# The first attention of a four-layer block and its input loads, rewritten as one pipeline over batches

## The chip, the cores and the metric

The kernel runs on one core of a Trainium2 chip. A time is the device time of one execution in microseconds (us), the lower the better. The core's engines are TensorE (PE; PEld is its weight load), VectorE (DVE), ScalarE (ACT), GpSimd (POOL) and SyncE (SP). SP computes nothing here, it issues DMAs in order from one queue.

## The reference, cut to what matters

The block has four layers of cross-attention and feed-forward. Only the first attention and the load of its inputs are touched. `x` and `ctx_4096` are (8, 128, 512): 8 batches of 128 tokens. There are 32 query heads and 8 key heads of 16 columns, and four query heads share a key head.

```
q = layernorm(x) @ Wq;  k = ctx @ Wk;  v = ctx @ Wv      # 32, 8 and 8 heads of 16
scores = einsum('bhqd,bhkd->bhqk', q, k) * 16 ** -0.5
out = einsum('bhqk,bhkd->bhqd', softmax(scores), v)
x = x + out @ Wo
```

The products want nearly float32 accuracy. So each operand is split into two float16 halves (high, and low = value - high), and a product is three matmuls: high x high, high x low, low x high (`pair_matmul`, L64 to L69).

## The kernel before

The program is a row of stages with a barrier of all engines between them. Two of them matter here.

`load_and_split_context` (L107 to L148) loads the context, already turned, in four cuts of 512 KB and then all of `x` (2 MB) in one DMA (L119, L120). ScalarE writes the high halves (L138), VectorE the low ones (L145), and then takes the statistics of all eight batches of `x`. A barrier ends it.

`attention` with the plan `A0` (L232) is the second. It works in four turns `g`, one for each group of 8 query heads and 2 key heads; in a turn it goes through the 8 batches, so there are 32 steps. Turns 1 and 2 are a hardware loop (`all_turns`, L367). Each engine runs its own `step(g, i)`, and lags set the order: scores of batch i, turned probabilities of batch i-1, values mixed for i-2, output projection for i-3, addition to `x` for i-4. In numbers, per step of 8 heads (two units of 4 heads):

- keys are spread (L437): the 128 rows of a key bank are multiplied by `spread`, so that each head sees only its own 16 rows. VectorE makes `kb_hi`, GpSimd `kb_lo`, 128x1024 each;
- the scores are 3 matmuls of 128x512 for each unit; VectorE takes the maxima (L800), ScalarE the exponentials, head by head with a sum each (L704);
- the probabilities are turned by TensorE, in float32, 4 for each unit (L586), and come out of PSUM as two halves: high by ScalarE (L691), low by VectorE (L782);
- the values are mixed (24 matmuls of 16 columns), VectorE divides by the sums (L845), TensorE turns the result (L615), and its halves (L715, L824) are multiplied by that turn's 128 rows of Wo: one product of 512 columns, added to `x` (L808). So `x` is added to 32 times.

Weights are loaded and split turn by turn (SP: L449 to L454, four DMAs for each turn). The first DMA transposes of the program come in a later attention (`wide_attention`), where SP issues them for queries (L1102), keys (L1107) and probabilities (L1113).

Of the kernel before, what the change touches and what calls it, by code (L numbers as in the profile page):

```python
# [106 lines left out]
def load_and_split_context(K, x_in, ctx_t):  # L107

    nc = K.nc
    with ExitStack() as c:  # L110
        cn = c.enter_context(nc.sbuf_tensor("ctx_nat", [P, KT, B * P], F32))
        x_in_done, const_done = K.sem("x_in"), K.sem("const")
        cut_in = [K.sem(f"ctx_in{k}") for k in range(KT)]
        hi_done = Steps(K.sem("ctx_hi_done"), list(range(KT)))
        with nc.Block() as block:
            @block.sync
            def _(sp):
                for k in range(KT):
                    sp.dma_start(cn[:, k, :], ctx_t[k * P:(k + 1) * P, :]).then_inc(cut_in[k], 16)  # L119
                sp.dma_start(K.x[:, :, :], x_in.rearrange("b s d -> s b d")).then_inc(x_in_done, 16)  # L120
                sp.wait_ge(x_in_done, 16)

            @block.gpsimd
            def _(pool):
                pool.memset(K.ident[:, :], 0.0).then_inc(const_done, 1)
                pool.memset(K.ones[:, :], 1.0).then_inc(const_done, 1)
                pool.memset(K.half[:, :], -0.5).then_inc(const_done, 1)
                pool.memset(K.minus_one[:, :], -1.0).then_inc(const_done, 1)
                pool.wait_ge(const_done, 4)
                pool.affine_select(out=K.ident[:, :], in_=K.ident[:, :], compare_op=ALU.not_equal, fill=1.0,  # L130
                                   base=0, pattern=[[-1, P]], channel_multiplier=1).then_inc(const_done, 1)
                pool.wait_ge(const_done, 5)

            @block.scalar
            def _(act):
                for k in range(KT):
                    act.wait_ge(cut_in[k], 16)
                    act.activation(K.ctx_hi[:, k, :], cn[:, k, :], ACT.Copy).then_inc(hi_done.sem, 1)  # L138

            @block.vector  # L140
            def _(dve):
                for k in range(KT):
                    dve.wait_ge(cut_in[k], 16)
                    dve.wait_ge(hi_done.sem, hi_done.count(k))
                    dve.tensor_tensor(K.ctx_lo[:, k, :], cn[:, k, :], K.ctx_hi[:, k, :], ALU.subtract)  # L145
                dve.wait_ge(x_in_done, 16)
                for b in range(B):
                    K.take_stats(dve, b)  # L148


# [66 lines left out]
class Attention:  # L217


    def __init__(self, name, groups, heads, dim, blocks, rows, per_unit, key_tiles, value_dim, units, banks, plan, ahead):  # L220
        self.name, self.groups, self.heads, self.dim = name, groups, heads, dim
        self.blocks, self.rows = blocks, rows
        self.per_unit, self.units = per_unit, units
        self.key_tiles, self.value_dim = key_tiles, value_dim
        self.banks = banks
        self.plan, self.ahead = plan, ahead
        self.packed = name == "a0"
        self.normed = name == "a2"
# [4 lines left out]

A0 = Attention("a0", 4, 8, 16, 1, 128, 4, 1, 32, 2, dict(made=1, s=2, ot=1, pt=2, o=1, y=1), {
    0: [("k", 1)], 1: [("q", 0, 1)], 2: [("v", 1)], 2.5: ["wo"]}, {
    3.5: ["wk"], 4: ["wq"], 5: [("k", 0)], 6: [("q", 0, 0), "wv"], 7: [("v", 0)]})
A1 = Attention("a1", 4, 4, 96, 4, 96, 2, 2, 96, 2, dict(made=3, s=2, pt=1, o=1, y=1), {
# [4 lines left out]
A2 = Attention("a2", 8, 4, 128, 4, 128, 4, 1, 128, 1, dict(made=3, s=2, pt=1, o=1, y=1), {  # L242
    0: [("q", 2), ("qn", 3)], 1: [("v", 0), ("q", 3)], 2: [("qn", 4)], 2.5: [("wo", 0)],
    3: [("q", 4), ("qn", 5), ("wo", 1), ("qn", 6), ("wo", 2), ("v", 1), ("q", 5), ("wo", 3), ("qn", 7), ("k", 1)],
    3.5: [("q", 6), ("q", 7)]}, {
    3.5: ["wk"], 4: [("kn", 0), ("wq", 0)], 4.5: [("wq", 1)], 5: [("kn", 1), ("wq", 2)], 5.5: [("wq", 3)],
    6: [("qn", 0), ("qn", 1)], 6.5: ["wv"], 7: [("q", 0), ("k", 0), ("qn", 2)], 7.5: [("q", 1)]})


def attention(K, A, wq, wk, wv, wo, mask=None, qw=None, kw=None):  # L250

    nc, N, G, R, D = K.nc, A.name, A.groups, A.rows, A.dim
    T = B * P
    scale = float(D) ** -0.5
    nt = A.key_tiles * B
    lag_turn, lag_mix, lag_out, lag_add = 1, 2, 3, 4
    heads_of = lambda j: range(j * A.per_unit, (j + 1) * A.per_unit)  # L260
    is_turn = lambda g, n: isinstance(g, int) and g == n
    with ExitStack() as c:
        sb = lambda n, shape, dt: c.enter_context(nc.sbuf_tensor(f"{N}_{n}", shape, dt))
        pair = lambda n, shape: (sb(n + "_hi", shape, F16), sb(n + "_lo", shape, F16))
        sem = lambda n: K.sem(f"{N}_{n}")

        if A.packed:
            nq, nk, nv = (sb(n, [P, KT, w], F32) for n, w in (("nq", P), ("nk", A.value_dim), ("nv", A.value_dim)))
            no = sb("no", [P, 1, DIM], F32)
            spread = sb("spread", [P, A.heads, P], F16)  # L270
            kb = [pair(f"kb{i}", [P, A.heads, P]) for i in range(2)]
            o_nat = sb("o_nat", [P, P], F32)
        else:
            nq, nk, nv = (sb(n, [P, KT, w], F32) for n, w in (("nq", A.blocks * R), ("nk", R), ("nv", R)))
            no = sb("no", [R, A.blocks, DIM], F32)
        wq_p, wk_p = pair("wq", [P, KT, A.blocks * R]), pair("wk", [P, KT, R])
        wv_p, wo_p = pair("wv", [P, KT, A.value_dim]), pair("wo", [R, A.blocks, DIM])
        q_p, k_p, v_p = pair("q", [R, A.blocks, T]), pair("k", [R, nt * P]), pair("v", [P, nt, A.value_dim])
        probs = [sb(f"probs{i}", [P, A.units, 512], F32) for i in range(2)]

        normal = probs if A.packed else [sb(f"normal{i}", [P, A.units, 512], F32) for i in range(2)]
        negmax = [sb(f"negmax{i}", [P, A.heads], F32) for i in range(2)]
        recip = [sb(f"recip{i}", [P, A.heads], F32) for i in range(4)]
        total = [sb(f"total{i}", [P, A.heads], F32) for i in range(2)]
        pt_p = [pair(f"pt{i}", [P, A.units, 512]) for i in range(2)]
        o_p = pair("o", [R, A.blocks, P])
        if A.normed:
            mk = sb("mask", [P, P], F32)
            masked = [sb(f"masked{i}", [P, A.heads, P], F32) for i in range(2)]

            k_ss, k_r, q_ss, q_r = (sb(n, [P, w], F32) for n, w in
                                    (("k_ss", B), ("k_r", B), ("q_ss", B * A.heads), ("q_r", B * A.heads)))
            kn, qn = sb("kn", [P, B, P], F32), sb("qn", [P, 2, A.heads, P], F32)
            wcol, wqk = sb("wcol", [P, 2], F32), sb("wqk", [P, 1], F32)

        per_v = 4
        before_turn = [use for i in sorted(A.ahead) for use in A.ahead[i]]
        made = before_turn + [use for i in sorted(A.plan) for use in A.plan[i]]
        prep = [use for use in made if use[0] == "w" or use[0] in ("wq", "wo")]
        last_qkv = [use for use in prep if "wo" not in (use, use[0])][-1]  # L300
        last_wo = [use for use in prep if "wo" in (use, use[0])][-1]
        banked = [use for use in made if use not in prep]
        last_of = lambda kinds, half: [use for use in made if use[0] in kinds and (use in before_turn) == (half == 0)][-1]
        free_banks = iter(K.bank)
        take = lambda name, uses: Banks(K, f"{N}_{name}", [next(free_banks) for _ in range(A.banks[name])], uses)
        units = [(b, j) for b in range(B) for j in range(A.units)]
# [6 lines left out]
        if A.packed:  # L313
            ot_bank = take("ot", list(range(B)))
            every_bank.append(ot_bank)
# [47 lines left out]
        def all_turns(engine, step):  # L363

            for i in range(B):
                step(0, i)
# [2203 lines left out]
```

## Time and profile before

| | us |
|---|---|
| median of 3 runs | 1888.47 (1884.77 to 1889.16) |
| profiled execution, its own time | 1886.01 |
| its span, first to last instruction | 1884.3 |
| loads and context split, with barrier | 0 to about 19.2 |
| first attention up to the first maximum of scores | 19.2 to 51.4 |
| its 32 steps up to the last exponentials | 51.4 to about 258 |
| drain and barrier; the next stage's first VectorE work | 258 to 272.4 |
| everything after, not touched | 272.4 to 1884.3 |

The page gives each engine's busy time over the whole span (PE 1605.5 us, DVE 1178.5, ACT 796.8, POOL 608.8). The touched part is its first seventh, so the stretches and single rows are what to read. A row in order of time gives start, length, engine and line, what was written from what, and in brackets how long the engine had been idle and who ended that. "SPq" is a DMA being issued by SP: its length is the time that SP is held, not that of the transfer.

### The profile page before, as it was taken

To read this page: it belongs to the slowest core of one execution; us is meant where nothing else is said; L and a number is where in the kernel's file an instruction comes from. 1 tells how busy PE (TensorE), PEld (TensorE's weight loads), DVE (VectorE), ACT (ScalarE), POOL (GpSimd) and SP (SyncE) were. 2 spreads that over 40 slices of the span, in tenths; PEclk is the share of its full clock that TensorE was granted. 3 is DMA by queue.
4 is the path that set the end of the run, shared out by engine and by line. 5 is a ranking of instruction groups with operands and counts; after the bars stand their busy time and mean duration, and the time that the engine had idled before them with its cause. 6 is when DMAs were issued, how large, how long until landed. Compare 5 with 4: busy or idle time off the path is not lost. (4 is left out here: it accounts for less than half of the span.)

```text
span 1884.3 us, 31640 instructions
## 1 busy us (share of the span) xinstructions
PE 1605.5 (85%) x10796; PEld 897.1 (48%) x10796; DVE 1178.5 (63%) x2287; ACT 796.8 (42%) x2789; POOL 608.8 (32%) x517
## 2 busy tenths in 40 slices
PE   2888955899899999996699999999996769449997
PEld 1455532344366666652365555555552334234443
DVE  5677776434455555564588887888777879771212
ACT  2676755211044334332176666666652312251111
POOL 2333328100014443450066666666653001220000
PEclk9899976799999999998799999999999779869998
DMA  2000012000034442240264546565433000200001
GB/s 103 15 15 15 1 69 92 0 0 0 1 83 93 78 78 62 57 79 26 94 141 104 132 106 129 105 133 107 99 77 91 34 1 1 62 31 0 0 0 45
DMA packets 265956, 111.07 MB, mean 59 GB/s; under 512 B 232305, under 2 KB 248497, under 8 KB 265698
## 3 DMA queue, kind: packets, MB, share of 16 engines
q1 hardware_dynamic: 265826, 109.40, 25.1%
q8 instruction: 74, 1.21, 0.3%
q14 instruction: 56, 0.46, 0.1%
HBM read 52.74 MB, written 2.10 MB: 29 GB/s over the span
## 5 line engine op out<-in xcount | busy, mean ns | idle before, releaser
L67 PE MATMUL bank<-a_wo_hi,a_o_hi 128*128 128x512 f16 (+1 forms) x416 | 159.1, 382 | 19.1 <-DVE a_o_lo L824 10.4
L1443 POOL TENSOR_TENSOR a_recip<-a_total,minus_one 128x4 f32<-128x4 f32 x96 | 97.8, 1019 | 195.9 <-ACT a_probs L1295 195.9
L69 PE MATMUL bank<-a_wo_hi,a_o_lo 128*128 128x512 f16 (+1 forms) x416 | 159.1, 383 | 0.0
L68 PE MATMUL bank<-a_wo_lo,a_o_hi 128*128 128x512 f16 (+1 forms) x416 | 159.1, 382 | 0.0
L1450 POOL TENSOR_TENSOR a_normal<-a_probs,a_recip 128x512 f32<-128x512 f32 x128 | 155.4, 1224 | 7.5
L1435 POOL TENSOR_TENSOR a_q_ss<-a_q_ss,half 128x4 f32<-128x4 f32 x64 | 89.2, 1393 | 189.3 <-DVE a_q_ss L1365 95.5
L1295 ACT ACTIVATE a_probs<-a_masked,a_negmax 128x128 f32<-128x128 f32 x256 | 99.6, 390 | 94.8 <-DVE a_negmax L1340 94.8
L1306 ACT ACTIVATE a_o_hi<-bank 128x512 f16<-128x512 f32 (+1 forms) x96 | 57.1, 595 | 180.6 <-PE bank L69 180.4
L1558 ACT ACTIVATE f_h_hi<-f_h 128x512 f16<-128x512 f32 (+1 forms) x50 | 31.5, 630 | 205.8 <-DVE f_h L1579 144.1
L67 PE MATMUL bank<-xn_hi,f_w_hi 128*128 (+1 forms) x288 | 110.9, 385 | 8.2 <-PEq L1511 8.2
L437 POOL TENSOR_TENSOR a_kb_lo<-a_k_lo,a_spread 128x1024 f16<-128x1024 f16 x32 | 69.4, 2169 | 150.1 <-PE bank L69 139.5
L68 PE MATMUL bank<-xn_lo,f_w_hi 128*128 (+1 forms) x288 | 110.7, 384 | 0.0
L69 PE MATMUL bank<-xn_hi,f_w_lo 128*128 (+1 forms) x288 | 110.5, 384 | 0.0
L1350 DVE TENSOR_TENSOR a_o_lo<-bank,a_o_hi 128x512 f16<-128x512 f32 (+1 forms) x96 | 65.6, 683 | 67.3 <-ACT a_o_hi L1306 67.3
L67 PE MATMUL bank<-a_wq_hi,xn_hi 128*128 128x512 f16 x256 | 97.3, 380 | 0.4 <-DVE a_qn L1370 0.4
L68 PE MATMUL bank<-a_wq_lo,xn_hi 128*128 128x512 f16 x256 | 97.3, 380 | 0.0
L69 PE MATMUL bank<-a_wq_hi,xn_lo 128*128 128x512 f16 x256 | 97.3, 380 | 0.0
L1570 DVE SCALAR_TENSOR_TENSOR f_h<-bank,f_act 128x512 f32<-128x512 f32 (+1 forms) x22 | 15.2, 691 | 127.8 <-PE bank L69 127.8
L1295 ACT ACTIVATE a_probs<-bank,a_negmax 128x256 f32<-128x256 f32 x128 | 59.0, 473 | 79.3 <-DVE a_negmax L1342 79.3
L704 ACT ACTIVATE a_probs<-bank,a_negmax 128x128 f32<-128x128 f32 x256 | 90.1, 393 | 4.6 <-DVE a_negmax L800 4.5
L1337 DVE TENSOR_TENSOR a_masked<-bank,a_mask 128x512 f32<-128x512 f32 x64 | 44.2, 690 | 73.0 <-PE bank L69 73.0
L67 PE MATMUL bank<-f_w_hi,f_h_hi 128*128 (+2 forms) x200 | 77.0, 385 | 10.2 <-DVE f_h_lo L1583 9.7
(338 smaller groups left out, 4894.4 us busy)
## 6 DMA issues: line engine op xcount, KB each, us to landing
a_nq<-in_L_xattn_Wq SPq DMA_DIRECT2D x8, 1024.0 KB, 5.7
a_no<-in_L_xattn_Wo SPq DMA_DIRECT2D x8, 1024.0 KB, 6.0
f_n<-in_L_ffn_w SPq DMA_DIRECT2D x1, 3584.0 KB, 11.6
f_n<-in_L_ffn_w2t SPq DMA_DIRECT2D x1, 3584.0 KB, 20.2
a_nq<-in_L_xattn_Wq SPq DMA_DIRECT2D x4, 768.0 KB, 4.8
a_no<-in_L_xattn_Wo SPq DMA_DIRECT2D x4, 768.0 KB, 5.7
f_words<-in_L_ffn_w SPq DMA_DIRECT2D x2, 1280.0 KB, 6.0
ctx_nat<-in_ctx_t SPq DMA_DIRECT2D x4, 512.0 KB, 4.9
```

Of the source, the lines that this page charges most:

```text
L67: pe.matmul(out, lh, rh, start=start, stop=False)
L68: pe.matmul(out, lh, rl, start=False, stop=False)
L69: return pe.matmul(out, ll, rh, start=False, stop=stop)
L437: engine.tensor_tensor(kb[b % 2][half][:, :, :], k_p[half][:, b * P:(b + 1) * P].unsqueeze(1).to_broadcast([P, A.heads, P]), spread[:, :, ...
L704: m = act.activation(probs[i % 2][:, j, n * w:(n + 1) * w], src, ACT.Exp, bias=negmax[i % 2][:, h:h + 1], accum_out=total[i % 2][:, h:h + 1])
L1295: m = act.activation(probs[s % 2][:, h, :], src, ACT.Exp, bias=negmax[s % 2][:, h:h + 1], accum_out=total[s % 2][:, h:h + 1])
L1306: act.activation(o_p[s % 2][0][:, :, :], o_bank[s][0:R, :].rearrange("p (h q) -> p h q", h=H), ACT.Copy).then_inc(ohi_done.sem, 1)
L1337: dve.tensor_tensor(masked[s % 2][:, :, :], s_bank[(s, 0)][:, :].rearrange("p (h n) -> p h n", h=H), mk[:, :].unsqueeze(1).to_broadcast([P ...
L1350: dve.tensor_tensor(o_p[s % 2][1][:, :, :], o_bank[s][0:R, :].rearrange("p (h q) -> p h q", h=H), o_p[s % 2][0][:, :, :], ALU.subtract).th ...
L1435: pool.tensor_tensor(r[:, :], r[:, :], K.half[:, 0:n], ALU.pow).then_inc(root_done.sem, 1)
L1443: pool.tensor_tensor(recip[s % 2][:, :], total[s % 2][:, :], K.minus_one[:, :], ALU.pow).then_inc(recip_done.sem, 1)
L1450: m = pool.tensor_tensor(normal[s % 2][:, t, :, :], probs[s % 2][:, :, t * P:(t + 1) * P], by, ALU.mult)
```

## The change

The two stages become one function, `first_attention`. It has no turns: all weights are loaded once, and a flat list of steps `t` from -15 to 89 goes over 64 units (8 batches of 8 units, a unit is 4 heads). Each engine walks the same steps and does at step t what the offsets say (`at(t, offset)` is the batch for which the offset falls on t, `live(t - lag)` the unit).

- Load: `x` and context come batch by batch (256 KB each); GpSimd, which has the constants and the square roots as before, now also takes the low halves of rows, context, keys, probabilities and heads.
- q and k: the host permutes Wq. A batch's queries come out of one bank of 128x512, its keys out of 128x128, which VectorE masks into two copies with alternate 16 rows (`keep`). SP then stacks the halves: 12 DMAs of 32 partitions put (high, low, high) of q below one another in 96 rows of `q3`, 12 more put (high, high, low) of k in `k3`. One matmul over 96 rows then is the whole three-part product of a score.
- Softmax: the values get a 17th column of ones, so that mixing also gives the sums; the exponentials keep none. Probabilities are split before they are turned: high by VectorE (five of eight units) or GpSimd (three of eight), low by GpSimd. SP turns both halves in one DMA transpose (128 x 1024 of float16), as it does for the normalised rows and for the heads.
- Output: all 32 heads of a batch are gathered, divided, split and turned by DMA, and the projection of 4 products goes into one bank. `x` is added to 8 times.

The diff, cut to its core:

```diff
-def load_and_split_context(K, x_in, ctx_t):
...
-def attention(K, A, wq, wk, wv, wo, mask=None, qw=None, kw=None):
...
+def first_attention(K, x_in, ctx_t, keep_in, wq, wk, wv, wo):
...
+    NORM, XHI, XLO, CTX = -15, -15, -13, -12
+    QPROJ, QSPLIT, KPROJ, KMASK, KSPLIT, VPROJ, VSPLIT = -9, -5, -10, -8, -8, -4, -3
+    PHI, PLO, MIX = 2, 2, 7
+    DIVIDE, OSPLIT, OUT, ADD = 11, 17, 22, 26
+    FIRST, END = -15, TOTAL + ADD
...
+    PS, PB = 6, 10
...
+        by_vector = lambda t: t % UNITS not in (2, 5, 7)
...
+                def stack_queries(b):
+                    sp.wait_ge(q_bank.freed(b), q_bank.n_drained(b))
+                    scored(b)
+                    for m in range(4):
+                        for third, half in enumerate((0, 1, 0)):
+                            sp.dma_start(q3[b % 2][32 * third:32 * third + 32, m, :, :].rearrange("p g n -> p (g n)"),
+                                         q_hl[b % 2][32 * m:32 * m + 32, half, :]).then_inc(q3_in[b % 2], 16)
...
+                def turn_probs(t):
+                    sp.wait_ge(plo_done.sem, plo_done.count(t))
+                    if t >= PB:
+                        sp.wait_ge(mixed.sem, mixed.count(t - PB))
+                    sp.dma_start_transpose(p_t[t % PB][:, :, :, :].rearrange("p a h n -> p (a h) n"),
+                                           p_hl[t % PS][:, :, :].rearrange("p a n -> p (a n)")).then_inc(p_in[t % PB], 16)
...
+                for t in range(FIRST, END):
+                    for b in at(t, XLO):
+                        turn_queries_in(b)
+                    for b in at(t, KSPLIT):
+                        stack_keys(b)
...
+                    for u in live(t - PLO):
+                        turn_probs(u)
+                    for b in at(t, OSPLIT):
+                        turn_heads(b)
+                    for b in at(t, QSPLIT):
+                        stack_queries(b)
...
+                def scores(t):
+                    b, i = t // UNITS, t % 4
+                    if t % UNITS == 0:
+                        landed(pe, q3_in, b, 12)
+                        landed(pe, k3_in, b, 12)
+                    pe.wait_ge(s_bank.freed(t), s_bank.n_free(t))
+                    for mm in range(2):
+                        m = 2 * (t % UNITS // 4) + mm
+                        r = pe.matmul(s_bank[t][:, 256 * mm:256 * mm + 256], q3[b % 2][:, m, i, :], k3[b % 2][:, m, :, :],
+                                      start=True, stop=True)
...
+                def high_of_probs(t):
+                    dve.wait_ge(s_bank.freed(t), s_bank.n_drained(t))
+                    if t >= PS:
+                        dve.wait_ge(p_in[(t - PS) % PB], 16 * ((t - PS) // PB + 1))
+                    dve.tensor_copy(p_hl[t % PS][:, 0, :], probs[t % PS][:, :]).then_inc(phi_done[0].sem, 1)
...
+                def low_of_probs(t):
+                    high_ready(pool, t)
+                    pool.tensor_tensor(p_hl[t % PS][:, 1, :], probs[t % PS][:, :], p_hl[t % PS][:, 0, :],
+                                       ALU.subtract).then_inc(plo_done.sem, 1)
...
-        load_and_split_context(K, a["x"], a["ctx_t"])
...
-    attention(K, A0, *(a[f"L0_xattn_{w}"] for w in ("Wq", "Wk", "Wv", "Wo")))
+    first_attention(K, a["x"], a["ctx_t"], a["keep"], *(a[f"L0_xattn_{w}"] for w in ("Wq", "Wk", "Wv", "Wo")))
```

SP before, from the start of the program (L119: context, L449 to L454: the first turn's weights):

```order
L119 DMA ctx_nat<-in_ctx_t 128x1024 x4
L120 DMA x_state<-in_x 128x8x512
L115 UNCONDITIONAL_BRANCH
L442 UNCONDITIONAL_BRANCH
L449 DMA a_nk<-in_L_xattn_Wk 128x4x32
L450 DMA a_nv<-in_L_xattn_Wv 128x4x32
L451 DMA a_nq<-in_L_xattn_Wq 128x4x128
L454 DMA a_no<-in_L_xattn_Wo 128x512
```

SP now, one batch's worth in the middle (`a_p_hl`: halves of the probabilities, `a_o_hl`: of the heads, `a_xn_hl`: of the normalised rows, `a_q_hl` and `a_k_hl`: of q and k):

```order
L300 DMA_TRANSPOSE a_p_t<-a_p_hl 128x8x128 x2
L307 DMA_TRANSPOSE a_o_t<-a_o_hl 128x8x128
L300 DMA_TRANSPOSE a_p_t<-a_p_hl 128x8x128
L272 DMA_TRANSPOSE a_xn_t<-a_xn_hl 128x8x128
L300 DMA_TRANSPOSE a_p_t<-a_p_hl 128x8x128
L285 DMA a_q<-a_q_hl 32x512 x12
L300 DMA_TRANSPOSE a_p_t<-a_p_hl 128x8x128
L314 DMA a_ctx<-in_ctx_t 128x4x128
L300 DMA_TRANSPOSE a_p_t<-a_p_hl 128x8x128 x3
L293 DMA a_k<-a_k_hl 32x256 x12
```

Behind four loads for each turn there now stand, for each batch, 10 transposes, 24 short copies and a load.

VectorE before, one step of 8 heads (L437 spreads keys, L845 divides, L824 and L782 are low halves):

```order
L800 TENSOR_REDUCE a0_negmax0<-bank1 128x4
L800 TENSOR_REDUCE a0_negmax0<-bank2 128x4
L808 SCALAR_TENSOR_TENSOR x_state<-bank6,x_state 128x512
L824 TENSOR_TENSOR a0_o_lo<-bank7,a0_o_hi 128x128
L782 TENSOR_TENSOR a0_pt1_lo<-bank3,a0_pt1_hi 128x512
L782 TENSOR_TENSOR a0_pt1_lo<-bank4,a0_pt1_hi 128x512
L437 TENSOR_TENSOR a0_kb1_hi<-a0_k_hi,a0_spread 128x1024
```

VectorE now, three steps of a middle batch (L558: high half of the probabilities, L564 and L568: divide, L576: high half of the heads, L529: low half of q):

```order
L551 TENSOR_REDUCE a0_negmax1<-bank1 128x4
L576 CAST a0_o_hl0<-a0_o_nat0 128x512
L558 CAST a0_p_hl0<-a0_probs0 128x512
L551 TENSOR_REDUCE a0_negmax2<-bank2 128x4
L580 SCALAR_TENSOR_TENSOR x_state<-bank6,x_state 128x512
L98 BN_STATS stats<-x_state 128x6
L558 CAST a0_p_hl1<-a0_probs1 128x512
L551 TENSOR_REDUCE a0_negmax3<-bank0 128x4
L564 RECIPROCAL a0_recip0<-bank3 128x16
L568 TENSOR_TENSOR a0_o_nat1<-bank3,a0_recip0 128x256
L529 SCALAR_TENSOR_TENSOR a0_q_hl1<-bank5,a0_q_hl1 128x512
```

For each unit the maxima stay; the low halves out of PSUM and the spreading are gone, and copies from SBUF to SBUF have come.

## Rows read from the trace of the kernel before

**Rows 1.** Table of stretches: length, busy us (count) by engine, clock, DMA share.

```profile
0.00:19.20 19.20, 0.00 (x0) 0.00 (x0) 9.74 (x12) 5.51 (x5) 0.93 (x9) 1.00 0.60 218
19.20:51.40 32.20, 16.28 (x108) 8.95 (x109) 15.56 (x38) 7.49 (x21) 9.36 (x7) 0.90 0.12 29
51.40:258.00 206.60, 174.64 (x1777) 102.69 (x1775) 155.84 (x333) 147.14 (x657) 65.15 (x30) 0.93 0.04 10
258.00:272.40 14.40, 7.79 (x68) 3.95 (x68) 8.05 (x17) 2.22 (x7) 0.04 (x1) 0.57 0.00 0
```

**Rows 2.** Order of time, VectorE: start, us, work, idle before it.

```profile
14.15 4.84 DVE L98 BATCH_NORM_STATS2 stats<-x_state 128x6 f32<-128x512 f32 x8 [3.33 <-DMA x_state<-in_x]
...
22.09 5.89 DVE L179 TENSOR_SCALAR a_n_xn<-x_state,a_n_mv,a_n_rstd 128x512 f32<-128x512 f32 x8 [2.14 <-POOL a_n_rstd L186]
```

**Rows 3.** Order of time at the stage's end, VectorE.

```profile
270.63 0.69 DVE L98 BATCH_NORM_STATS2 stats<-x_state 128x6 f32<-128x512 f32 x1
272.40 0.64 DVE L176 BATCH_NORM_AGGREGATE f_n_mv<-stats 128x2 f32<-128x6 f32 x8 [1.08 <-PEq L103]
```

**Rows 4.** Order of time at the stage's end, TensorE.

```profile
264.34 0.61 PE L67 MATMUL bank<-a_wo_hi,a_o_hi 128*128 128x512 f16 x1 [1.04 <-DVE a_o_lo L824]
264.74 0.63 PE L68 MATMUL bank<-a_wo_lo,a_o_hi 128*128 128x512 f16 x1
...
265.67 0.17 PE L68 MATMUL bank<-a_v_lo,a_pt_hi 128*128 128x16 f16 x1
265.69 0.17 PE L69 MATMUL bank<-a_v_hi,a_pt_lo 128*128 128x16 f16 x1
```

**Rows 5.** Order of time, SP queue: three DMA transposes in a row.

```profile
1353.84 1.23 SPq L1102 DMA_TRANSPOSE a_q_t<-a_q_nat  x1
1355.16 1.23 SPq L1107 DMA_TRANSPOSE a_k_t<-a_k_nat  x1
1356.48 1.26 SPq L1113 DMA_TRANSPOSE a_p_t<-a_p_nat  x1
```

**Rows 6.** Order of time, SP queue: short transfers behind one another.

```profile
859.70 0.32 SPq L1848 DMA_DIRECT2D f_nbias<-in_L_ffn_b  x1
860.08 0.36 SPq L1849 DMA_DIRECT2D f_had<-in_hadamard  x1
860.48 0.42 SPq L1850 DMA_DIRECT2D f_na<-in_L_ffn_lora_A  x1
```

**Rows 7.** Order of time, SP queue: a transfer behind four large loads.

```profile
921.52 0.51 SPq L1087 DMA_DIRECT2D a_no<-in_L_xattn_Wo  x1
922.07 1.08 SPq L1092 DMA_DIRECT2D a_mask<-in_mask_1x1xSxS_ff  x1
```

**Rows 8.** Groups by shape, VectorE, 51.4 to 258 us: total, mean ns.

```profile
L800 DVE TENSOR_REDUCE a_negmax<-bank 128x4 f32<-128x512 f32 x64 | 41.1, 680 | 4.0 <-PE bank L69 3.6 <-issue 0.3
```

**Rows 9.** Groups by shape, VectorE, from 300 us on.

```profile
L1370 DVE TENSOR_TENSOR a_kn<-bank,a_k_ss 128x256 f32<-128x256 f32 x32 | 13.6, 425 | 4.7
...
L1985 DVE TENSOR_SCALAR f_te<-f_tw 128x512 int32<-128x512 int32 x12 | 5.1, 427 | 0.4
```

**Rows 10.** Groups by shape, GpSimd, from 300 us on.

```profile
L1453 POOL CAST a_p_nat<-a_normal 128x512 f16<-128x512 f32 x64 | 43.1, 673 | 4.1
...
L2283 POOL TENSOR_TENSOR x_weight<-x_picked,x_recip 128x512 f32<-128x512 f32 x8 | 8.3, 1039 | 74.9 <-DVE x_recip L2257 74.9
```

**Rows 11.** One line's instructions, VectorE: ns min/median/max; a kb_hi product.

```profile
L437 DVE TENSOR_TENSOR a_kb_hi<-a_k_hi,a_spread x32: 676/682/2108, 49.1 to 251.6; 128x1024 f16<-128x1024 f16 x32
```

**Rows 12.** The same for a weight's low half in the later attention.

```profile
L1400 DVE SCALAR_TENSOR_TENSOR a_wk_lo<-a_nk,a_wk_hi x12: 545/1110/1529, 523.2 to 1308.5; 128x512 f16<-128x512 f32 x8, 128x384 f16<-128x384 f32 x4
```

**Rows 13.** DMA issues: KB, median us from issue to landing.

```profile
a_p_t<-a_p_nat SPq DMA_TRANSPOSE x96, 3.2
...
a_nq<-in_L_xattn_Wq SPq DMA_DIRECT2D x4, 256.0 KB, 3.5
```

More of the change, by code:

```diff
@@ L264, in attention @@
         pair = lambda n, shape: (sb(n + "_hi", shape, F16), sb(n + "_lo", shape, F16))
+        ring_of = lambda n, k, shape, dt: [sb(f"{n}{i}", shape, dt) for i in range(k)]
         sem = lambda n: K.sem(f"{N}_{n}")
[L267 to L303, printed above, removed]
@@ L304, in attention @@
-        free_banks = iter(K.bank)
-        take = lambda name, uses: Banks(K, f"{N}_{name}", [next(free_banks) for _ in range(A.banks[name])], uses)
-        units = [(b, j) for b in range(B) for j in range(A.units)]
-        ring, s_bank, pt_bank = take("made", banked), take("s", units), take("pt", units)
-        o_bank, y_bank = take("o", list(range(B))), take("y", list(range(B)))
-        early_units = range(min(A.units, A.banks["pt"]))
-        late_units = range(len(early_units), A.units)
@@ new lines, in first_attention @@
+        units, batches, halves = list(range(TOTAL)), list(range(B)), [(b, hf) for b in range(B) for hf in range(2)]
+        take = lambda name, banks, uses: Banks(K, f"{N}_{name}", banks, uses)
+        s_bank, o_bank = take("s", K.bank[0:3], units), take("o", K.bank[3:5], halves)
+        q_bank, y_bank = take("q", K.bank[5:6], batches), take("y", K.bank[6:7], batches)
+        kv_bank = take("kv", K.bank[7:8], [(kind, b) for b in batches for kind in "kv"])
+        x_here, ctx_here = [sem(f"x_in{b}") for b in batches], [sem(f"ctx_in{b}") for b in batches]
@@ new lines, in first_attention @@
+        w_here = {k: [sem(f"{k}_in{i}") for i in range(4 if k == "wq" else 1)] for k in nat}
+        pieces = [("wk", 0)] + [("wq", i) for i in range(4)] + [("wv", 0)] + [("wo", i) for i in range(4)]
+        whi_done, wlo_done = Steps(sem("whi"), pieces), Steps(sem("wlo"), pieces)
+        per_batch = lambda n: Steps(sem(n), batches)
+        per_unit = lambda n: Steps(sem(n), units)
+        stats_done, mean_done, root_done = sem("stats"), sem("mean"), sem("root")
+        xn_done, xhi_done, xlo_done, chi_done, clo_done = (per_batch(n) for n in ("xn", "xhi", "xlo", "chi", "clo"))
@@ new lines, in first_attention, with landed @@
+        phi_done = [Steps(sem(f"phi{n}"), [u for u in units if by_vector(u) == (n == 0)]) for n in range(2)]
+        high_ready = lambda engine, t: engine.wait_ge(phi_done[not by_vector(t)].sem, phi_done[not by_vector(t)].count(t))
+        weights_at = lambda t: [use for use, when in zip(pieces, WEIGHTS) if when == t]
+        def landed(engine, sems, b, n=1):
+            engine.wait_ge(sems[b % 2], 16 * n * (b // 2 + 1))
+        def weight(use):
+            kind, i = use
+            if kind == "wo":
+                piece = lambda t: t[:, i, :]
+            elif kind == "wq":
+                piece = lambda t: t[:, :, i * P:(i + 1) * P]
+            else:
+                piece = lambda t: t[:, :, :]
+            return [piece(p) for p in w_p[kind]], piece(nat[kind])
@@ L535, in turned_queries @@
-                def turned_queries(g, use):
-                    b = use[1]
-                    normalised(g, ("qn", b), use)
-                    for h in range(A.heads):
-                        m = pe.transpose(ring[use][:, h * P:(h + 1) * P], qn[:, b % 2, h, :], K.ident[:, :])
-                    return m
-                makers = {"kn": keys_by_row,
-                          "k": turned_keys if A.normed else keys, "v": values, "q": turned_queries if A.normed else queries,
-                          "qn": queries_by_row}
@@ new lines, in _ @@
+                for t in range(FIRST, END):
+                    for u in live(t):
+                        scores(u)
+                    for u in live(t - MIX):
+                        mix(u)
+                    for k in range(KT):
+                        for b in at(t, OUT + k):
+                            project_out(b, k)
+                    for i in range(4):
+                        for b in at(t, QPROJ + i):
+                            queries(b, i)
+                    for b in at(t, VPROJ):
+                        values(b)
+                    for b in at(t, KPROJ):
+                        keys(b)
@@ L730, in _, with high_of_weight @@
-                for use in before_turn[:without_xn]:
-                    high(0, use)
-                norm.high(act)
-                if A.normed:
-                    act.wait_ge(wqk_done, 1)
-                for use in before_turn[without_xn:]:
-                    high(0, use)
-                all_turns(act, step)
+                def high_of_weight(use):
+                    kind, i = use
+                    dst, src = weight(use)
+                    act.wait_ge(w_here[kind][i if kind == "wq" else 0], 16)
+                    act.activation(dst[0], src, ACT.Copy, scale=WS).then_inc(whi_done.sem, 1)
@@ new lines, in _ @@
+                pool.wait_ge(const_done, 4)
+                pool.affine_select(out=K.ident[:, :], in_=K.ident[:, :], compare_op=ALU.not_equal, fill=1.0,
+                                   base=0, pattern=[[-1, P]], channel_multiplier=1).then_inc(const_done, 1)
+                for t in range(FIRST, END):
+                    for u in live(t - PHI):
+                        if not by_vector(u):
+                            high_of_probs(u)
+                    for b in at(t, XLO):
+                        low_of_rows(b)
+                    for b in at(t, CTX):
+                        low_of_context(b)
+                    for u in live(t - PLO):
+                        low_of_probs(u)
+                    for b in at(t, OSPLIT):
+                        low_of_heads(b)
+                    for part, (b0, b1, when) in enumerate(ROOTS):
+                        if t == when:
+                            roots(part)
+                    for b in at(t, KSPLIT):
+                        low_of_keys(b)
```

871 lines of the change are left out of this document (317 added, 554 removed), and 4 rows, old and new, of the table A1.

## The prediction

> **What bounds the kernel now.** Read first the table of stretches [rows 1]: the two stages that the change rewrites take 0 to 272.4 us. In the first 19.2 us TensorE has nothing to do; up to 51.4 us it is half busy; the 32 steps run from 51.4 to 258 (6.5 us a step, 3.2 for each unit of 4 heads); then comes a drain of 14.4. In the steps no engine is full: PE 85% of the stretch, DVE 75%, ACT 71%, and the DMA share is 0.04. So the steps are limited by TensorE's work and the chain through its in-order queue; the DMA side is idle. The start is a chain too: `x` lands whole, then eight statistics, then 2.14 us for the roots on GpSimd [rows 2]. The stage ends with statistics at 270.63, and the next stage's first VectorE work is at 272.40 [rows 3]. Everything from there on is the same code with the same inputs, so the forecast is 272.4 less the new place of that instruction.
>
> **What the change takes away, engine by engine, for a batch of 8 units.** TensorE: a score product is one matmul of 96 rows instead of three, the float32 turns are gone, the output is projected once and not four times. What is left in columns is scores 16x256, q 48x128, k and v 24x128, output 12x512, together 19,456. At the lower of the clock's two levels 512 columns take 0.40 us (264.34 to 264.74) and a short mixing product 0.025 (265.67 to 265.69) [rows 4]. That makes 15.2 us and 96 x 0.025 = 2.4: at most 17.6 us a batch, even at half clock. ScalarE was busy 147 us in the steps with more work than it keeps (it loses the high halves out of PSUM and the sums), so under 18 us a batch.
>
> **SP's queue, the new work.** It held almost nothing. Now there are for each batch 8 transposes of probabilities, one of rows, one of heads, 24 short copies and a load of context. A transpose holds SP 1.23 us, start to start 1.32 [rows 5]; 10 make 13.2. A short copy of 32 partitions from SBUF to SBUF stands nowhere in this trace. The nearest rows in shape are three small loads in a row, 0.38 and 0.40 us start to start [rows 6]. Behind large loads one holds SP 0.51 (0.55 to the next start), and the one after that 1.08 [rows 7]. I take 0.40, as the copies stand in runs of twelve small ones; the ends are 0.36 and 1.12 (below nothing isn't possible, a queue must issue them). So 24 x 0.40 = 9.6, and 0.5 for the load: **23.3 us a batch**.
>
> **VectorE** for each batch: 8 maxima at 0.68 [rows 8] = 5.4; four more of 512 columns (low half of q, addition, two statistics) 2.7; the mask and two divisions of 256 columns at 0.425, 1.3; the normalised rows and 8 copies from SBUF to SBUF (five probabilities, rows, context, heads) at 0.43 [rows 9], 3.9; small ones 0.9. Together 14.2. The copy's price is that of a one-source operation; the bound is the two-source 0.68 (2 us a batch more). **GpSimd**: 8 low halves of probabilities and 3 others at 1.04, three high halves at 0.67 [rows 10], keys 0.55: 14.0. These two get in each other's way. `kb_hi` took 2.11 us once where 0.68 is usual, with `kb_lo` on GpSimd beside it [rows 11], and a weight's low half has a median of 1.11 and up to 1.53, where the form takes about 0.7 [rows 12]. With GpSimd some 65% busy a copy meets it often and waits half of a 1.04 us operation: 8 x 0.4 = 3.2 on VectorE, 17.4 in all. If each copy waited out a whole one, 22.5. The weights' low halves (10 pieces of 0.7, once instead of in four turns) lie in the start, where VectorE waits for `x` anyway; without that cover they would be 7 us.
>
> The Trainium skill (SBUF — State Buffer, Who interferes with whom) says that a copy in a two-port mode and a GpSimd instruction hold a shared port pair exclusively and that the second fully blocks. These rows agree in kind; by that rule the sum is the 22.5 above, still just under SP's 23.3.
>
> So **SP is the engine that sets the pace**, with VectorE 6 us a batch behind it. Can the others run ahead of it? `high_of_probs` of unit t waits for the transpose of t-6, and scores of a batch wait for its stacks, issued 5 steps before. After SP's run of 12 for q it has six probabilities, 12 copies for k and a transpose of heads to issue, 14.7 us, before it needs the first unit of the new batch; that unit needs about 3 us to land and 4 to come through. So SP doesn't starve in the middle.
>
> **The sum, in the new stage's own time.** The first rows of `x` are a quarter megabyte, issued at 0.8 and landing 3.5 later [rows 13]: 4.3. Statistics 0.85, the root of one column 1.5 (at most the 2.14 for eight), normalising 0.43, high 0.43, low on GpSimd 1.04, and hand-overs: 8.9. SP turns them (10.2) and issues the second `x`, which lands at 13.7. VectorE stands in order at the wait for that load, and behind its statistics is queued the first batch's mask, on which ScalarE, GpSimd and then SP's whole stack of k wait; after statistics, roots and both halves of k it is 16.8. Stack of k 4.8, rows 1.3, stack of q 4.8: T0 = 28, with the first scores some 3 us later (before: 51.4).
> T0 to T1, the end of the second batch's q stack: loads 3.0, k 4.8, two probabilities 2.6, rows 1.3, q 4.8 = 16.5, so 44.5. Then six batches: 22.0 (no heads yet), 3 x 23.3, 22.8 (no context), 21.5 (no rows): 136, so 180.5. From there 14 probabilities and two heads, 21.1, so the last probability is issued at 200.3 and lands 3.2 later: 203.5. The engines need some 8 x 1.7 + 4 us for the last batch, and just keep up.
> The tail: mix 0.4, division 0.9, high 0.4, low 1.0, transpose 3.2, 12 output matmuls at 0.42 = 5.0 (the low clock of 0.57 in the drain [rows 1]), addition and statistics 1.4, barrier 1.1, gaps 0.3: 13.7. The next stage starts at 217.2 instead of 272.4, 55 less. The profiled execution took 1886.0 by its own clock, 2.5 under the median of the runs; that gives 1831, and with a microsecond for hand-overs on SP **1832 us**.
>
> **The rivals.**
> 1. *SP does not bind, VectorE with GpSimd does.* For it: if a run of twelve overlaps in the descriptor hardware, the copies cost next to nothing, and the engines go at 17.4. Against it: no row shows an issue under 0.32. First scores at 26, 8 x 17.4 = 139, end of the pipe 5, tail 14: 184, 88 less, 1798; with losses at the ring, 1800 to 1812.
> The Trainium skill (DMA: Bandwidth & Descriptors, Issuing engines are not separate DMA queues) says of the time that a sequencer takes to initiate a DMA that it is "usually small relative to the DMA itself". By that rule this rival would be the case. The transposes speak against it: 1.23 held of 3.2 to landing.
> 2. *The copies are dearer*, 0.55 each, as behind another load [rows 7]; or VectorE pays the port in full and both stall in turn. 192 x 0.15 = 29 more, 1861; with transposes held up now and then, 1870.
> 3. *Slower than before.* SP's queue backs up: transposes and copies share the DMA engines, and a copy behind a full queue costs what the mask's load did, 1.08 [rows 7]. Then 192 x 0.7 = 138 more, 1970. It decides from (55 / 192) + 0.40 = 0.69 us a copy on. Against it: that row stood behind 2.5 MB of loads, and a copy here moves 16 or 32 KB.
> 4. *The change doesn't do what it says*: the stages overlap less than written, and the gain comes from fewer instructions alone. If the start stayed at 51.4 as now, 20 us more: 1852, inside the range.
>
> **How the numbers follow.** SP as forecast (0.36 to 0.46 a copy, 1818 to 1845): 0.53. Rival 1, 0.15. Rival 2 with part of 4 (1845 to 1880): 0.20. About no change: 0.04. Rival 3: 0.08. The range 1800 to 1872 leaves out half of the first rival's tail below 1800 and the two slow cases, about 2 in 10. 0.3% of this time is 5.7 us, about what a measurement can tell from no change. Faster 0.88, same 0.04, slower 0.08.
>
> **What would show it.** In the profile after: the next stage's first statistics aggregate near 217; SP's stack copies 0.35 to 0.42 start to start, and hardly an idle gap in its queue from 28 to 200 us; VectorE and GpSimd waiting for a `a_p_t` transpose or for PE's scores at each batch's start; VectorE busy about 14 to 18 us in 23. First scores at 30. Wrong would be: SP idle between transposes, waiting for GpSimd's low halves (rival 1), copies over 0.5 us (rival 2), landings of 6 us and more (rival 3).

## The result: no gain, and the profile after

The changed kernel took 1896.57 us (median of 5 runs, 1893.64 to 1897.57), the kernel before 1887.88 beside it: a ratio of 1.0047, with an interval of 1.0037 to 1.0058. A second comparison (the last experiment) gave 1.0031 (1.0019 to 1.0043). By the ends of the two intervals it is slower by 4 to 11 us, where 1832 was forecast. The profiled execution took 1897.57 by its own clock, its span is 1895.8.

The table of stretches of the profile after, over the new stage (length, busy us and count of PE, PEld, DVE, ACT, POOL, then granted clock, DMA share and GB/s), answers to [rows 1]:

```profile
0.00:24.30 24.30, 6.63 (x84) 6.17 (x84) 13.26 (x24) 6.66 (x11) 10.85 (x25) 0.93 0.58 165
24.30:49.00 24.70, 9.24 (x87) 7.88 (x88) 12.19 (x20) 9.57 (x30) 7.84 (x7) 0.64 0.57 150
49.00:262.30 213.30, 107.18 (x1352) 75.88 (x1350) 89.25 (x184) 72.31 (x250) 109.09 (x109) 0.67 0.61 115
262.30:276.80 14.50, 8.64 (x48) 3.53 (x48) 3.88 (x7) 0.00 (x0) 1.15 (x1) 0.76 0.28 52
```

In the steps every computing engine is about half idle or more, though the instructions went away as the change says: in 213 us TensorE is busy for 107, GpSimd 109, VectorE 89, ScalarE 72. The DMA share is 0.61 where it was 0.04. The stage ends with these two rows of VectorE, to be held against [rows 3]:

```profile
274.88 0.69 DVE L98 BATCH_NORM_STATS2 stats<-x_state 128x6 f32<-128x512 f32 x1
276.85 0.64 DVE L132 BATCH_NORM_AGGREGATE f_n_mv<-stats 128x2 f32<-128x6 f32 x8 [1.28 <-PEq L103]
```

So the next stage starts at 276.85, not at 217.2 as forecast and not at 272.40 as before. The table of waits from 24 to 263 us (who waited for whom: us in total, times, longest) leads to the cause:

```profile
ACT a_probs L456 <- DVE a_negmax L551: 110.0, 51, 14.3
DVE a_negmax L551 <- PE bank L399: 97.3, 28, 14.0
...
PE bank L67 <- DMA a_p_t<-a_p_hl: 53.5, 20, 8.7
PE bank L399 <- DMA a_q<-a_q_hl: 51.9, 8, 7.3
```

ScalarE waits for VectorE's maxima, VectorE for TensorE's scores, and TensorE for transfers: once in each batch 6.5 us for the stack of q (line 399), and for turned probabilities. All these transfers are issued by SP. Here is its queue for one batch, in order of time (start, time it was held, count at the row's end; a row of several includes the short pauses between them):

```profile
110.03 7.50 SPq L285 DMA_DIRECT2D a_q<-a_q_hl  x12
117.63 1.25 SPq L300 DMA_TRANSPOSE a_p_t<-a_p_hl  x1
118.93 0.58 SPq L314 DMA_DIRECT2D a_ctx<-in_ctx_t  x1
119.62 5.54 SPq L300 DMA_TRANSPOSE a_p_t<-a_p_hl  x3
125.25 7.50 SPq L293 DMA_DIRECT2D a_k<-a_k_hl  x12
132.85 2.64 SPq L300 DMA_TRANSPOSE a_p_t<-a_p_hl  x2
135.54 1.33 SPq L307 DMA_TRANSPOSE a_o_t<-a_o_hl  x1
136.96 1.29 SPq L300 DMA_TRANSPOSE a_p_t<-a_p_hl  x1
138.34 1.29 SPq L272 DMA_TRANSPOSE a_xn_t<-a_xn_hl  x1
139.72 1.39 SPq L300 DMA_TRANSPOSE a_p_t<-a_p_hl  x1
141.21 9.00 SPq L285 DMA_DIRECT2D a_q<-a_q_hl  x12
```

No gap in it exceeds 0.12 us. A batch takes 31.2 us, of which 15 are the two runs of twelve copies; the next run took 9.0. The runs of q start at 24.3, 49.0, 78.6, 110.0, 141.2, 173.7, 204.5 and 232.5: 25 to 33 us apart, where 16.5 and then 21.5 to 23.3 was forecast. Summing SP's rows from 24.32 to 232.50 gives for each copy 0.68 us, start to start (0.40 forecast), for each transpose of probabilities 1.44 (1.32), and 5.2 us idle in 208, nearly all of it pauses of about 0.1 between two issues.

### The profile page after: what moved, and what is told of

It is laid out like the page before. It is cut to its first block and busy times, and to the rows that moved or that the text cites. A ratio compares the mean times of both kernels' runs of the same rounds, so it can differ in the third digit from the quotient of the medians.

```text
span 1895.8 us, 30325 instructions
## 1 busy us (share of the span) xinstructions
PE 1546.4 (82%) x10412; PEld 876.4 (46%) x10412; DVE 1107.8 (58%) x2121; ACT 722.4 (38%) x2391; POOL 663.1 (35%) x612
## 3 DMA queue, kind: packets, MB, share of 16 engines
q8 instruction: 75, 1.23, 0.3%
## 5 line engine op out<-in xcount | busy, mean ns | idle before, releaser
L67 PE MATMUL bank<-a_wo_hi,a_o_hi 128*128 128x512 f16 (+1 forms) x384 | 145.6, 379 | 8.4 <-DVE x_state L1132 8.4
L69 PE MATMUL bank<-a_wo_hi,a_o_lo 128*128 128x512 f16 (+1 forms) x384 | 145.5, 379 | 0.0
L68 PE MATMUL bank<-a_wo_lo,a_o_hi 128*128 128x512 f16 (+1 forms) x384 | 145.5, 379 | 0.0
L456 ACT ACTIVATE a_probs<-bank,a_negmax 128x128 f32<-128x128 f32 x256 | 72.8, 369 | 110.2 <-DVE a_negmax L551 110.0
L551 DVE TENSOR_REDUCE a_negmax<-bank 128x4 f32<-128x512 f32 x64 | 43.9, 686 | 97.3 <-PE bank L399 97.3
L648 POOL TENSOR_TENSOR a_p_hl<-a_probs,a_p_hl 128x512 f16<-128x512 f32 x64 | 75.0, 1177 | 65.4 <-DVE a_p_hl L558 64.0
```

Source lines behind the costliest of these rows:

```text
L67: pe.matmul(out, lh, rh, start=start, stop=False)
L68: pe.matmul(out, lh, rl, start=False, stop=False)
L69: return pe.matmul(out, ll, rh, start=False, stop=stop)
L456: m = act.activation(probs[t % PS][:, h * P:(h + 1) * P], s_bank[t][:, h * P:(h + 1) * P], ACT.Exp, bias=negmax[t % 4][:, h:h + 1])
L648: pool.tensor_tensor(p_hl[t % PS][:, 1, :], probs[t % PS][:, :], p_hl[t % PS][:, 0, :], ALU.subtract).then_inc(plo_done.sem, 1)
```

## Experiments

The diffs are against the changed kernel and cut to their core; `...` inside a line stands for what is left out of it. Where a time has no interval, it is that of one execution; the ten of one variant lay within 10 us of each other. "Stage" is the time at which SP issues the next stage's first load: 276.8 us in the changed kernel.

**What a copy costs by itself.** The groups stand behind the last stage. `bs` and `bd` are in SBUF, `far` is in DRAM.

```diff
+                for rows, cols in ((32, 512), (32, 256), (32, 128), (16, 512), (8, 512), (64, 512)):
+                    group([(bd[...], bs[...]) for i in range(min(8, 2 * P // rows))])
+                group([(bd[:, i, :], bs[:, 0, :]) for i in range(2)])
+                group([(bd[...], far[...]) for i in range(8)])
+                group([(far[...], bs[...]) for i in range(8)])
```

> The changed kernel, with groups of like transfers put on SP's queue before the output is stored, each group waited for before the next, all engines idle: eight copies SBUF to SBUF of 32 partitions x 512 f16, of 32 x 256, 32 x 128, 16 x 512, 8 x 512, four of 64 x 512, two of 128 x 512, eight of 32 x 512 from DRAM, eight of 32 x 512 to DRAM. Theory 1 (the price is intrinsic to a copy from SBUF to SBUF of 32 rows, whatever runs beside it): 0.60 to 0.70 us start to start for 32 x 512 here too, and 0.35 to 0.45 for the same rows from DRAM. Theory 2 (in the pipeline the queue is held up by transposes in the same DMA engines): 0.35 to 0.45 here for both. Within theory 1, a price by rows gives 16 rows at 0.4 or less and 128 rows over 1.5; a fixed price gives 0.6 for all; a price by bytes gives 32 x 128 at a quarter. The whole kernel some 40 to 80 us longer than without the groups.

SP's queue in order of time; the rows are 32 x 512, 32 x 256, 32 x 128, 16 x 512, 8 x 512, 64 x 512, 128 x 512, 32 x 512 from DRAM and to DRAM:

```profile
2494.82 5.00 SPq L2264 DMA_DIRECT2D bench_d<-bench_s  x8
2501.12 4.94 SPq L2264 DMA_DIRECT2D bench_d<-bench_s  x8
2507.29 4.94 SPq L2264 DMA_DIRECT2D bench_d<-bench_s  x8
2513.43 4.95 SPq L2264 DMA_DIRECT2D bench_d<-bench_s  x8
2519.64 5.38 SPq L2264 DMA_DIRECT2D bench_d<-bench_s  x8
2526.20 2.44 SPq L2264 DMA_DIRECT2D bench_d<-bench_s  x4
2530.10 1.13 SPq L2264 DMA_DIRECT2D bench_d<-bench_s  x2
2532.69 3.58 SPq L2264 DMA_DIRECT2D bench_d<-bench_far  x8
2537.70 3.55 SPq L2264 DMA_DIRECT2D bench_far<-bench_s  x8
```

The price belongs to the copy itself, and it follows neither rows nor bytes. With the rest of the core idle a copy from SBUF to SBUF takes 0.61 to 0.63 us of the queue, start to start, for 16, 32 and 64 rows and for 256 to 1024 bytes a row. The eight of 8 rows took 0.68 and the two of 128 rows 0.52; the first of a group is mostly the shortest, so two say little. With DRAM on either side the 32 x 512 takes 0.45. Transposes beside it are not needed for this price. Why the memories at the two ends make the difference, no run shows. The whole kernel took 2552 us, not 40 to 80 us more, and that is not the copies' doing, which are some 50 us: this one execution was granted the lower level of the clock most of the time. That makes it a second experiment. Its two stretches, the first stage and all the rest:

```profile
0.00:275.70 275.70, 144.69 (x1568) 102.24 (x1568) 119.06 (x234) 89.10 (x291) 128.05 (x142) 0.57 0.59 119
275.70:2550.30 2274.60, 2041.24 (x8826) 982.92 (x8844) 1001.62 (x1888) 638.36 (x2100) 533.50 (x471) 0.63 0.20 47
```

At a mean clock of 0.57 the new first stage ends at 275.7; at 0.69 it ended at 276.8. The rest takes 2275 us, with the copies in it, instead of 1619. TensorE doesn't bound this stage at either level.

**A third of the copies.**

```diff
-                        for third, half in enumerate((0, 1, 0)):
+                        for third, half in ((0, 0),):
 ...   the same for k
-                        r = pe.matmul(..., q3[b % 2][:, m, i, :], k3[b % 2][:, m, :, :],
+                        r = pe.matmul(..., q3[b % 2][0:32, m, i, :], k3[b % 2][0:32, m, :, :],
```

> The changed kernel with 8 of the 24 stack copies a batch: the thirds 1 and 2 are left out, and the score product takes 32 rows instead of 96 (two of the three partial products of the scores are left out). Theory 1 (SP's queue sets the pace, 0.65 us a copy): 16 x 0.67 = 10.7 us a batch off SP, which leaves it 20.5, so 60 to 85 us faster, 1812 to 1837. Rival (the pace is set by the engines and the lower clock, the copies lie beside it): within 15 us of the changed kernel, 1880 to 1897.

1808.9 us, stage 195.2: 82 us less for 128 copies less, 0.64 each. The rival is out: the kernel leaves out two of the three partial products of a score, but TensorE was half idle before. The time is 3 us below the range given.

**Twelve more.**

```diff
+                    for m in range(4):
+                        for third, half in enumerate((0, 1, 0)):
+                            sp.dma_start(spare[32 * third:..., m, :, :], wide_src[32 * m:..., half, :])
```

> The changed kernel with twelve further copies a batch of 32 x 512 from a spare tile into a spare tile, put on SP's queue behind the stack of q; nobody waits for their data but the next group of them. Theory 1 (SP's queue sets the pace): 8 x 12 x 0.63 = 60 us longer, about 1957. Rival (the pace is set by the engines): under 15 us longer.

1955.8 us, 59 more than the changed kernel, and the stage ends at 335.1, 58 later: 0.61 us for each of the 96. Between the two runs the pace follows the number of copies on SP's queue: 19.6 us a batch with 8 of them, 29.7 with 24, 36.9 with 36 (mean of seven batches, first run of q to last).

**The keys' copies from another queue.**

```diff
-                    for b in at(t, KSPLIT):
-                        stack_keys(b)
 ...
+                    for m in range(4):                      # ScalarE's block
+                        for b in at(t, KSPLIT + 1 + m):
+                            stack_keys(b, m)                # three act.dma_start
```

> The changed kernel with the twelve copies of k a batch issued from ScalarE's queue, three in each of four steps, instead of SP's. Theory 1 (SP's queue sets the pace by what it issues itself): SP has 23.3 us a batch left, ScalarE 9 to 13 of work and 7.5 of issues, so 8 x 7.6 = 60 us faster, about 1836. Rival A (what limits is shared by all queues, the DMA engines or their descriptor hardware): under 15 us faster. Rival B (the engines take over as the bound at 27 us a batch or more): 20 to 35 us faster.

1848.18 us (1845.76 to 1851.97), 0.979 of the kernel before (0.9770 to 0.9811), stage 227.0. The same bytes are moved, and 48 us are gone: it is the issuing queue that bounds, and two queues issue side by side. Of the rest, part went into dearer transposes, 1.51 us each for probabilities by the sum of SP's rows (3.5 us in the seven batches, the other transposes 2), and part into the loads of `x` and a wait behind them (3.6). DMA share and landings are up there too. The copies on ScalarE's queue, and the stretch of seven batches, read:

```profile
L479 ACTq DMA_DIRECT2D a_k<-a_k_hl x96: 514/612/1506, 15.3 to 181.9; - x96
22.70:183.90 161.20, 100.22 (x1239) 77.50 (x1240) 89.67 (x178) 70.31 (x239) 99.84 (x100) 0.68 0.79 146
```

(the first row is the duration in ns, least, median and most). 161.2 us are 23.0 a batch, which is the pace that the prediction had given to SP.

**Stacks by way of DRAM, 8 transfers a batch.**

```diff
+                    sp.dma_start(q_far[b % 2], q_hl[b % 2][:, :, :])
 ...   two steps later
+                    for third, half in enumerate((0, 1, 0)):
+                        sp.dma_start(q3[b % 2][32 * third:32 * third + 32, :, :, :],
+                                     q_far[b % 2].rearrange("(m p) h n -> p m h n", m=4)[:, :, half, :])
```

> The changed kernel with each stack made through DRAM: the whole q or k tile is stored there by one transfer, and two steps later three loads, one for each third of 32 partitions x 4 x 512 (or 256), fill the stack: 8 transfers a batch on SP's queue instead of 24. Theory 1 (SP's queue sets the pace by the number of its transfers): 10 x 1.32 + 8 x 0.5 + 0.5 = 17.7 us a batch left, at which the DMA engines (16.4 us of busy time a batch in the run with one third of the copies) and the computing engines take over, at 19 to 21 us; 1800 to 1818. Rival A (the stored and loaded bytes, or landings from DRAM, hold the scores up): 1840 to 1875. Rival B (a shared limit other than the queue): within 15 us of the changed kernel.

1824.92 us (1818.40 to 1828.15), 0.9664 of the kernel before (0.9631 to 0.9697), stage 204.8. This is the fastest kernel of the study that computes everything. It is 7 us above the range: the pace is 20.7 us a batch, SP is held for 17.1 of it and idles 3.6, for GpSimd's low halves and for stores to land (one wait for the store of k is 7.0 us by itself). The stretch of seven batches:

```profile
22.60:167.80 145.20, 91.12 (x1243) 71.85 (x1240) 89.30 (x178) 71.59 (x246) 101.10 (x100) 0.77 0.92 183
```

**The forecast's own price, made true.** 24 loads of 32 partitions from DRAM, and two stores.

```diff
-                        sp.dma_start(q3[...], q_hl[b % 2][32 * m:32 * m + 32, half, :])
+                        sp.dma_start(q3[...], q_far[b % 2][32 * m:32 * m + 32, half, :])
```

> As the last one, but the stack is filled from DRAM by the same twelve transfers of 32 partitions as in the changed kernel: 24 loads and 2 stores a batch. In the row of transfers alone a load of this shape was 0.42 us on SP and 0.46 start to start, a copy from SBUF to SBUF 0.59 and 0.63. Theory 1 (the prediction's sum was right but for the price): 13.2 + 26 x 0.46 + 0.5 = 25.7 us a batch instead of 31, so 40 to 48 us faster than the changed kernel, 1848 to 1857. Rival (24 transfers cost in the pipeline what the DMA engines make them, wherever they come from): within 15 us of the changed kernel.

1883.8 us, stage 263.9: 13 us less, not 40 to 48. By the time alone this is the rival's case, within 15 us. The trace decides against its reason: the load did come at its price, median 0.42 held and 0.49 start to start in the queue, and 168 of them save 32 us in seven batches. But the two stores take 1.2 us a batch, the first q run starts 2.2 us later, and SP, which had idled 5.2 us in seven batches, now idles 18.7, of which one wait for the store of k is 5.1. The table of SP's waits from 60 to 185 us:

```profile
SPq L314 <- POOL a_p_hl L666: 8.4, 11, 1.3
SPq L293 <- DMA a_q_far<-a_q_hl: 2.6, 2, 2.2
SPq L321 <- POOL a_o_hl L671: 2.2, 2, 1.1
```

I read it so: a unit comes through the chain of scores, maximum, exponential and two halves in its own time, and SP's fixed order has it wait there when the stacks are quicker. No run tested the order. The sum of a queue's issues is a lower bound of its pace, not the pace.

**GpSimd's three copies undone.**

```diff
-        by_vector = lambda t: t % UNITS not in (2, 5, 7)
+        by_vector = lambda t: True
```

> The changed kernel with all eight high halves of probabilities copied by VectorE (GpSimd's three copies undone). Theory 1 (SP's queue sets the pace, VectorE and GpSimd wait for it): the same within 5.7 us, 1891 to 1902. Rival (the two engines' work or their shared port sets the pace): 5 us or more either way, up to 8 x 3 x 0.5 = 12 slower.

1894.04 us (1888.04 to 1897.82), 1.003 of before (1.0016 to 1.0044): the same as the changed kernel. Who copies the high halves has no price while both engines are half idle.

> The kernel by way of DRAM with all eight high halves copied by VectorE. With SP's queue relieved, the engines stand near the bound: if VectorE is the next one, 8 x 3 x 0.5 = 12 us slower than by way of DRAM with the three on GpSimd; if GpSimd with the port is, some 5 to 15 faster; if the DMA engines or SP still are, the same within 5.

The same edit upon the kernel by way of DRAM: 1825.5 us against 1824.9, stage 206.6 against 204.8. Moving these copies has no price even there, so the work of neither engine is the next bound by itself.

**More traffic from another queue.**

```diff
+                    for b in at(t, 1):                      # ScalarE's block
+                        act.wait_ge(spare_in, 16 * b)
+                        act.dma_start(spare[:, :, :], wq.rearrange("(k p) n -> p k n", p=P))
```

> The changed kernel with one further load of 1 MB from DRAM for each batch, issued from ScalarE's queue into a spare tile; SP's queue is as it was. At the 385 GB/s of the output's store it is some 2.7 us of all 16 DMA engines. Theory 1 (SP's own queue sets the pace, the DMA engines are 0.52 to 0.65 busy and have room): within 8 us of the changed kernel. Rival (the DMA engines set the pace): 15 to 22 us longer.

1922.15 us, stage 302.1: 25 us longer, and my expectation was wrong. The load holds ScalarE's queue for 0.38 us only. It is SP's queue that shows it: the transposes of probabilities, and three in a row around such a load (issued at 126.81):

```profile
L301 SPq DMA_TRANSPOSE a_p_t<-a_p_hl x64: 1244/1284/7296, 43.9 to 285.8; - x64
...
126.18 8.23 SPq L301 DMA_TRANSPOSE a_p_t<-a_p_hl  x3
```

Behind seven of the eight loads (issued from 59.7 on) one transpose holds SP for 4.2 to 7.3 us; in the changed kernel the longest is 2.75, right behind the load of context at 118.93. The median is as before, but their mean is 1.86 us start to start where it was 1.44 (sum of the rows over seven batches): 50 x 0.42 = 21 us. So a queue is not on its own: while a large load of another queue is under way, SP is held up to 7.3 us at a transpose. That would fit the dearer transposes of the fourth experiment too, and the 0.12 us that they cost above my sum; neither was tested.

> The kernel by way of DRAM with the same further load of 1 MB for each batch. There the DMA share is 0.86 to 1.03 in the steps. If the DMA engines are what bounds it now, most of 8 x 2.7 = 22 us is added, 12 to 22; if it is SP's queue or the computing engines, under 8.

1840.8 us, stage 221.3: 16 longer, in the range given for the DMA engines. SP is held 19 us longer there in seven batches and idles 7 less (17.9 instead of 25.2). But as the kernel with SP full lost 25 to the same load, this doesn't tell whether the kernel by way of DRAM is bound by the DMA engines or by SP. That stays open.

**Where the other 4 us are.** The stage itself ends 4.4 us later than before, the kernel 8.7.

> The kernel before, unchanged, for its profile. The stages behind the first took 1611.9 us in its profile and 1612.0 to 1619.0 in those of the changed kernel and its variants, although their code is the same. If the change slows them in some way, before again 1612 or less; if it is the granted clock of one execution or another, anywhere in 1610 to 1620.

> The changed kernel, unchanged, for the ratio and a second profile. First stage 275 to 278 us; the stages behind it 1612 to 1619, as in its variants. The ratio to before between 1.003 and 1.006, so that some 4 of the 8 us stand in the stage itself and the rest is open.

The kernel before again took 1886.2 us, the changed kernel again 1894.1 (median of 6; 1.0031 of before, as expected). Their stretches, the kernel before first:

```profile
0.00:268.80 268.80, 193.21 (x1952) 113.10 (x1952) 189.02 (x401) 162.26 (x689) 75.77 (x47) 0.94 0.09 26
268.80:1884.50 1615.70, 1411.13 (x8844) 781.87 (x8844) 989.21 (x1887) 634.62 (x2100) 533.52 (x471) 0.93 0.28 64
```

```profile
0.00:275.10 275.10, 132.67 (x1568) 94.66 (x1568) 118.95 (x234) 88.87 (x291) 128.97 (x141) 0.66 0.59 120
275.10:1893.20 1618.10, 1412.86 (x8844) 781.89 (x8844) 988.80 (x1887) 634.40 (x2100) 534.07 (x471) 0.93 0.28 64
```

The stages behind the first took 1611.9 and 1615.7 us before, 1619.0 and 1618.1 after, and 1612.0 to 1619.0 in nine variants at the usual clock. TensorE's busy time moves with it (1405 to 1415 us). A difference of a few us there is within what one kernel shows from one execution to the next; that the change causes part of it isn't excluded by four profiles. The stage itself took 268.8 and 272.4 before, 276.8 and 275.1 after.

## Why the prediction was wrong, step by step

- **What bounds the kernel before, and what goes away.** Right: TensorE's, ScalarE's and VectorE's busy time shrank as worked out. VectorE was busy for 12.4 us a batch (86.6 us in seven) against 17.4 forecast, or 14.2 without the port. The port's share is small: the copy of probabilities has a median of 0.42 us and a mean of 0.50, so 0.1 each and not 0.4. The case of 22.5, each copy waiting out a whole GpSimd operation, did not come: the longest copy took 1.17.
- **SP sets the pace.** Right, and nearly without a gap, as forecast; rival 1 is out. The trace also decides on the rule of the Trainium skill that stood beside it (DMA: Bandwidth & Descriptors, Issuing engines are not separate DMA queues). A copy holds its sequencer for 0.59 us of 1.8 to landing, a transpose for 1.28 of 3.3: a third or more, and not small.
- **The price of a copy: the step that failed.** "I take 0.40, as the copies stand in runs of twelve small ones." The rows it rests on [rows 6] are three loads from DRAM, of 2, 64 and 32 KB. Bytes and rows hardly have a price here, and the memories at the two ends have: 0.45 with DRAM at one end, 0.62 within SBUF, and 0.68 in the pipeline, where the median held is the same 0.59 and a few are longer, up to 2.03. 192 x 0.28 = 54 us. The copies of q, and the transposes (ns, least, median and most):

```profile
L285 SPq DMA_DIRECT2D a_q<-a_q_hl x96: 508/591/2032, 24.3 to 239.7; - x96
...
L300 SPq DMA_TRANSPOSE a_p_t<-a_p_hl x64: 1241/1284/2752, 43.6 to 260.9; - x64
```

- **The transposes.** 1.44 instead of 1.32: 64 of them, 8 us. The median held is 1.28 instead of 1.23, and a few long ones make the rest; that the traffic beside them causes these is likely by the run with more loads, but not shown for this kernel.
- **The sum.** Prologue to the end of the first q stack 32.8 instead of 28; from there to the end of the last one 207.5 instead of 152.5; from there to the next stage 36.6 instead of 36.7. The construction holds within a few us, and with 0.68 and 1.44 put in, its 217.2 becomes 217.2 + 54 + 8 = 279, against 276.8 measured.
- **The rivals.** Rival 3 named this queue and its break-even, 0.69 us a copy; the measured 0.68 lies on it, and so does the result, about no gain. Its mechanism, a backed-up queue, is not what raised the price; the run with more loads shows that the mechanism exists. Its 138 more is (1.12 - 0.40) x 192; the 192 x 0.7 that it names is 134. Rival 2 stopped at 0.55. I had bounds of 0.36 and 1.12 for a price that counts 192 times, and gave the neighbourhood of the break-even a chance of 0.04 and all above it 0.08. That is the second fault: a term with such ends is worth 146 us of range, and it was the forecast's largest unknown.
- **TensorE at the low clock** was rightly no term: the clock was 0.67 in the steps, and in the execution with 0.57 over the whole stage the stage ended at 275.7.

## What to carry to other kernels

Count what a queue has to issue, in a table of kinds and prices, before moving layout work from engines to DMAs; for transfers of the sizes tried here (8 to 128 KB) the bytes hardly matter, their number does. A price is taken from a row with the same memories at both ends, and where there is none, the range is the whole distance between the bounds. If such a queue is full, make fewer and larger transfers (1825 us here) or split them between queues (1848) before touching the engines.

## What the runs showed of the hardware

- A copy from SBUF to SBUF holds SP for 0.59 us (0.62 start to start) from 16 x 512 to 64 x 512 f16, and for 32 x 128 too; 8 x 512 took 0.62 (0.68). With DRAM at one end 32 x 512 took 0.42 (0.45).
- SP and ScalarE issue such copies side by side, each at its own pace: 0.59 and 0.61 us.
- A 1 MB load issued by ScalarE holds SP up, at its transposes: 4.2 to 7.3 us behind seven of eight such loads, where 1.28 is the median.
- One of the fourteen profiled executions ran mostly at the lower clock: 0.627 on average and 2552 us. Nothing in the edit, which stands behind all the computation, explains it, and it was not run again.
